# A GRU step on one Trainium2 core: gates r and z in banks of their own, fp32 products for the newest terms, and fp32 moving operands of 4 columns

## The reference

```
def step(h, xs):
    xzt, xrt, xht = xs
    z = jax.nn.sigmoid(xzt + h @ U_z + vz)
    r = jax.nn.sigmoid(xrt + h @ U_r + vr)
    hh = jnp.tanh(xht + r * h @ U + vh)
    h_new = (1.0 - z) * h + z * hh
    return (h_new, h_new)
h0 = jnp.zeros((seq.shape[0], U.shape[0]), seq.dtype)
xs = (jnp.swapaxes(xz, 0, 1), jnp.swapaxes(xr, 0, 1), jnp.swapaxes(xh, 0, 1))
_, out_t = jax.lax.scan(step, h0, xs)
```

## Time and profile before

| What | us |
|---|---|
| median of 3 runs | 760.3 |
| span of the profiled execution, first to last instruction | 755.7 |
| median of the runs less that span | 4.6 |
| PE busy, of that span | 640.4 |
| DVE busy | 461.1 |
| ACT busy | 324.6 |
| POOL busy | 178.0 |

### The profile page before, as it was taken

The page is one execution under the profiler, slowest core; times in us unless marked ns, Lnnn a source line. Parts: engine busy times, 40 slices in busy tenths (PEclk is TensorE's granted clock), DMA queues, the critical chain, the costliest instruction groups (busy, mean ns, idle before and its releaser), DMA issues.

```text
span 755.7 us, 26078 instructions
## 1 busy us (share of the span) xinstructions
PE 640.4 (85%) x7909; PEld 528.5 (70%) x7909; DVE 461.1 (61%) x3362; ACT 324.6 (43%) x1253; POOL 178.0 (24%) x789
## 2 busy tenths in 40 slices
PE   5998677656788888988889898889888889999995
PEld 4445566545677877877778787778777667877774
DVE  1536344343267777777777777777767556777663
ACT  2356434434145546455555555464544222322321
POOL 1023222221033232232232332322311001111110
PEclk9999967899589999999999999999999999999997
DMA  8022222222212221222212221212210000000000
GB/s 221 9 85 76 85 88 79 92 79 79 76 40 67 74 69 65 67 71 68 71 64 65 74 64 65 74 64 67 72 62 3 2 2 2 10 6 3 4 6 8
DMA packets 43965, 43.06 MB, mean 57 GB/s; under 512 B 5500, under 2 KB 43656, under 8 KB 43784
## 3 DMA queue, kind: packets, MB, share of 16 engines
q1 hardware_dynamic: 43328, 40.75, 16.6%
q10 hardware_dynamic: 584, 1.64, 0.6%
HBM read 20.95 MB, written 21.43 MB: 56 GB/s over the span
## 4 chain that ended last, share of the span: by engine, by line
PE 54%; DVE 14%; DMA 14%; issue 9%; ACT 7%; SPq 1%; DVEq 1%; ACTq 0%; POOLq 0%; POOL 0%
DMA skew<-e_sb 13%; PE bank L622 12%; PE bank L635 12%; PE bank L423 7%; PE bank L407 6%; DVE s_sb L845 3%; ACT hh L765 3%; PE bank L440 2%; DVE g L996 2%; DVE q L988 2%; ACT oT L651 2%; PE bank L455 2%; PE bank L527 2%; PE bank L457 2%; PE bank L453 2%
## 5 line engine op out<-in xcount | busy, mean ns | idle before, releaser
L355 POOL COPY x_nat<-d 128x4 f32 (+1 forms) x256 | 53.5, 209 | 395.7 <-DVE d L1001 395.7
L635 PE MATMUL bank<-q,uc 128*128 128x54 f32 (+1 forms) x512 | 106.1, 289 | 43.3 <-DVE q L988 40.8
L635 PEld LDWEIGHTS bank<-q,uc 128*128 128x128 f32 x512 | 77.7, 190 | 90.3 <-DVE q L988 85.6
L622 PE MATMUL bank<-g,uw 128*128 128x54 f16 (+1 forms) x2560 | 119.1, 189 | 3.6 <-DVE g L996 3.6
L755 ACT ACTIVATE trz<-bank 128x8 f32<-128x8 f32 x256 | 45.5, 178 | 167.9 <-PE bank L622 167.6
L622 PEld LDWEIGHTS bank<-g,uw 128*128 128x128 bf16 x2560 | 103.6, 97 | 17.1 <-DVE g L996 7.9
L622 PE MATMUL bank<-b,uw 128*128 128x54 f16 (+1 forms) x2560 | 110.1, 188 | 0.0
L651 ACT ACTIVATE e_sb<-bank 128x132 f32<-128x132 f32 (+1 forms) x256 | 84.2, 382 | 57.6 <-DMA skew<-e_sb 55.5
L622 PEld LDWEIGHTS bank<-b,uw 128*128 128x128 bf16 x2560 | 108.1, 103 | 1.0 <-issue 0.2
L765 ACT ACTIVATE hh<-bank 128x4 f32<-128x4 f32 x256 | 44.5, 174 | 135.7 <-PE bank L635 131.3
L996 DVE TENSOR_TENSOR g<-z,hh 128x4 f16<-128x4 f32 x256 | 41.9, 164 | 97.5 <-ACT hh L765 97.5
(11 more groups left out here) (133 smaller groups left out, 1054.4 us busy)
## 6 DMA issues: line engine op xcount, KB each, us to landing
skew<-e_sb SPq DMA_DIRECT2D x128, 159.5 KB, 2.7
pos<-skew SPq DMA_DIRECT2D x128, 128.0 KB
wkv_sb<-in_L_attn_Wkv ACTq DMA_DIRECT2D x1, 1024.0 KB, 8.3
x_nat<-in_x SPq DMA_DIRECT2D x1, 512.0 KB, 4.6
wq_sb<-in_L_attn_Wq ACTq DMA_DIRECT2D x1, 512.0 KB, 5.3
wo_sb<-in_L_attn_Wo SPq DMA_DIRECT2D x1, 512.0 KB, 7.3
out<-y_out SPq DMA_DIRECT2D x8, 64.0 KB
ffn_nat<-in_L_ffn_w_gate SPq DMA_DIRECT2D x1, 256.0 KB
```

The costliest lines, as they stand in the source:

```text
L622: ins = mm(out_, uw[:, gate, use, j, :], operand, start=False, stop=True, skip_group_check=True)
L635: mm(c_cols(k, n), uc[:, :], st["q8"][:, now, 0:n], start=False, stop=True, skip_group_check=True).then_inc(c_pre, 1)
```

## The change

Gate r now lies in bank 0, gate z in bank 1, the candidate in bank 2, for all 16 steps of a period. Gate z is one fp32 product of its U with the whole state d8. Gate r is five fp16 products of the older term b as before, and one fp32 product with g8. g1 and g2 are gone, with their two DVE instructions; tanh is taken of r and z apart, each with its own semaphore. The moving operands of the three fp32 products of a step (g8, d8, q8) have 4 columns, while the five products with b keep 54 or 60. The zero products go to bank 2, with widths as before. The setting of a bank to its biases (seed) is split in three and placed between the DVE instructions of a step, and input products of r and z are issued between the products with b and `first_window`.

```diff
-        parts = sb("parts", [128, 2, 3, D], BF16)
-        uw = sb("uw", [128, 2, 2, 3, D], BF16)
+        parts = sb("parts", [128, 3, D], BF16)
+        uw = sb("uw", [128, 3, D], BF16)
+        u32 = sb("u32", [128, 2, D])
...
-        def rz_cols(k, gate=0, n=2 * B):
-            at = (k % BLOCK * 2 + gate) * B
-            return bank[k // BLOCK][:, at:at + n]
-        def c_cols(k, n=B):
-            return bank[2][:, k * B:k * B + n]
+        def pre_cols(gate, k, n=B):
+            return bank[gate][:, k * B:k * B + n]
...
-                    for use, name, ok in ((1, "b", (b1_ok, b2_ok)), (0, "g", (g1_ok, g2_ok))):
-                        if name == "g":
-                            first_window(i, k, groups, tiles, last)
-                        for low in range(2):
-                            pe.wait_ge(ok[low], t + 1)
-                            for gate in range(2):
-                                ins = product(rz_cols(k, gate, n), gate, use, st[f"{name}{low + 1}"][:, before, 0:n], low)
-                    ins.then_inc(rz_pre, 1)
+                    NR, NZ, NC = B, B, B
+
+                    pe.wait_ge(b1_ok, t + 1)
+                    for j in range(3):
+                        mm(pre_cols(0, k, n), uw[:, j, :], st["b1"][:, before, 0:n], start=False, stop=True, skip_group_check=True)
+                    pe.wait_ge(b2_ok, t + 1)
+                    for j in range(2):
+                        mm(pre_cols(0, k, n), uw[:, j, :], st["b2"][:, before, 0:n], start=False, stop=True, skip_group_check=True)
+                    gate_inputs(i, k, last)
+                    first_window(i, k, groups, tiles, last)
+                    pe.wait_ge(g8_ok, t + 1)
+                    mm(pre_cols(0, k, NR), u32[:, 0, :], st["g8"][:, before, 0:NR], start=False, stop=True,
+                       skip_group_check=True).then_inc(r_pre, 1)
+                    pe.wait_ge(d8_ok, t + 1)
+                    mm(pre_cols(1, k, NZ), u32[:, 1, :], st["d8"][:, before, 0:NZ], start=False, stop=True,
+                       skip_group_check=True).then_inc(z_pre, 1)
                     main_window(i, k, groups, tiles, last)
                     pe.wait_ge(q8_ok, t + 1)
-                    mm(c_cols(k, n), uc[:, :], st["q8"][:, now, 0:n], start=False, stop=True, skip_group_check=True).then_inc(c_pre, 1)
+                    mm(pre_cols(2, k, NC), uc[:, :], st["q8"][:, now, 0:NC], start=False, stop=True, skip_group_check=True).then_inc(c_pre, 1)
...
-                    act.wait_ge(rz_pre, t + 1)
-                    act.activation(trz[:, now, :, :].rearrange("p g b -> p (g b)"), rz_cols(k), ACT.Tanh, scale=0.5).then_inc(trz_ok, 1)
+                    act.wait_ge(r_pre, t + 1)
+                    act.activation(trz[:, now, 0, :], pre_cols(0, k, B), ACT.Tanh, scale=0.5).then_inc(tr_ok, 1)
+                    act.wait_ge(z_pre, t + 1)
+                    act.activation(trz[:, now, 1, :], pre_cols(1, k, B), ACT.Tanh, scale=0.5).then_inc(tz_ok, 1)
```

More of the change, by code:

```diff
@@ L593, in main_window, with gate_inputs @@
                 if not groups[0][0]:
-                    free = bank[1 - k // BLOCK] if k not in (1, 9) else bank[3] if groups[1][0] else bank[7]
                     n = FILLER // 2 if any(s_ in TILE_MAIN for _, s_ in tiles_at(i, k, tiles)) else FILLER
-                    mm(free[:, 0:n], uw[:, 0, 0, 0, :], zeros[:, 0:n], start=(k in (1, 9)), stop=True, skip_group_check=True)
+                    mm(bank[2][:, 0:n], uw[:, 0, :], zeros[:, 0:n], start=False, stop=True, skip_group_check=True)
+                if k == 4:
+                    inputs(i, 1, 2)
+                if k == 15 and not last:
+                    inputs(i + 1, 0, 2)
+            def gate_inputs(i, k, last):
                 if k == 2:
@@ L599, in main_window @@
                     inputs(i, 1, 0)
+                if k == 3:
                     inputs(i, 1, 1)
-                if k == 4:
-                    inputs(i, 1, 2)
                 if k == 14 and not last:
@@ L764, in period @@
                     act.wait_ge(c_pre, t + 1)
-                    act.activation(st["hh"][:, now, :], c_cols(k), ACT.Tanh).then_inc(hh_ok, 1)
+                    act.activation(st["hh"][:, now, :], pre_cols(2, k), ACT.Tanh).then_inc(hh_ok, 1)
             periods(act, period)
@@ L817, in _ @@
             for n, item in enumerate(KQV):
-                if n % 2 == 1 and n // 2 < 13:
+                if n % 2 == 1 and n // 2 < 8:
                     split_u(n // 2)
@@ L973, in window @@
                     tile_stage(tau, step)
-                if k == 1 or (k == 9 and not last):
-                    seed(0 if k == 9 else 1)
             def period(i, groups, tiles, last):
@@ L983, in period @@
                     tr, tz = trz[:, now, 0, :], trz[:, now, 1, :]
-                    d8 = st["d8"][:, before, :]
+                    d8 = st["d8"][:, before, 0:B]
                     stt = dve.scalar_tensor_tensor
-                    dve.wait_ge(trz_ok, t + 1)
+                    dve.wait_ge(tr_ok, t + 1)
                     dve.wait_ge(d8_ok, t + 1)
                     stt(s["q8"], tr, 1.0, d8, ALU.add, ALU.mult).then_inc(q8_ok, 1)
+                    seeds = k == 1 or (k == 9 and not last)
+                    if seeds:
+                        seed(0 if k == 9 else 1, 0)
+                    dve.wait_ge(tz_ok, t + 1)
+                    dve.tensor_scalar(s["z8"], tz, 1.0, SPLIT, ALU.add, ALU.mult).then_inc(z8_ok, 1)
+                    stt(s["b8"], tz, -1.0, d8, ALU.add, ALU.mult).then_inc(b8_ok, 1)
                     stt(s["b1"], tz, -1.0, d8, ALU.add, ALU.mult).then_inc(b1_ok, 1)
-                    stt(s["b8"], tz, -1.0, d8, ALU.add, ALU.mult).then_inc(b8_ok, 1)
-                    dve.tensor_scalar(s["z8"], tz, 1.0, SPLIT, ALU.add, ALU.mult).then_inc(z8_ok, 1)
+                    if seeds:
+                        seed(0 if k == 9 else 1, 1)
                     dve.wait_ge(b8_ok, t + 1)
+                    dve.wait_ge(b1_ok, t + 2)
                     dve.tensor_tensor(s["b2"], s["b8"], s["b1"], ALU.subtract).then_inc(b2_ok, 1)
```

72 lines of the change are left out of this document (32 added, 40 removed).

## The result

The changed kernel takes 1008.97 us in the median of 4 runs (1007.1 to 1009.98), the kernel before 761.01 us in its 4 (759.01 to 762.62): a ratio of 1.3276, 95% interval [1.3237, 1.3316]. The profiled execution has a span of 1005.3 us.

What follows compares the result with a forecast made beforehand. Before, late steps were bound by the chain, with DVE also holding odd steps beside attention. At 1.2 GHz, 204.8 + 572.0 + 212.0 + 14.2 = 1003 us of span, with 4.6 us more 1008 us; range 850 to 1070.

Steps and rivals of the forecast that it cites:

- The clock: In the recurrence: starts at 1.2 GHz and, with the change, doesn't rise to 2.4 GHz, or not for long; chance 0.74.
- The count of columns: On PE: a recurrence step streams 1296 columns before, 318 after; with attention beside it, 3,080 become 2,100.
- the first rival: In the recurrence: the clock stays at or comes back to 2.4 GHz and the kernel is faster, 712 us; chance 0.10.
- the cold entry: At the recurrence's start: either kernel enters at 1.2 GHz, since attention runs dry ahead of it.
- slower steps keep the clock low: In the recurrence: steps at 1.2 GHz are slower and so emptier, against the clock holding beside attention.
- The price at 1.2 GHz: In the recurrence: 3.25 us a step beside attention and 2.65 late, for a span of 1003 us.
- heads, projection and inputs: On PE beside attention: 6.8 us a period, some 1 us of it in gaps, adding 0.36 us a step.
- PE sets the steps: Beside attention at 1.2 GHz: PE's own work is longer than the 2.12 us chain, 3.23 us odd, 2.58 even.
- the price of the first rival: In the recurrence at 2.4 GHz: 16 us less in late steps, 32 us less beside attention, from 760.3 to 712 us.
- I take nothing: On ACT beside attention: the second tanh, from nothing to 0.18 us a step, is put at no cost.
- the cover for z's tanh and b2: Behind r's product: z's tanh and its DVE readers are covered by the 0.43 us to the candidate's tanh; late b2 costs nothing.
- the other end: On ACT beside attention: the second tanh's upper cost, 176 x 0.18 = 32 us.

Runs made afterwards that it cites:

- e1: The changed kernel with its three fp32 moving operands 54 or 60 columns wide again: 811.53 us, 1.0677 of the kernel before.
- e3: The kernel before with all its operands 4 columns wide instead of 54 and 60: 919.08 us, 1.2131 of the kernel before.
- e6: As e5, with the three fp32 moving operands 54 or 60 columns wide again: 778.25 us, 1.0239 of the kernel before.
- e7: The kernel before with operands of 27 and 30 columns, half as wide: 784.39 us, 1.0322 of the kernel before.
- e5: The changed kernel with zero products ahead of the recurrence, in even steps beside attention and late steps, two more in each of the first six: 1055.36 us.
- e9: The changed kernel with z's and b's operands 100 or 128 wide, zero products at entry and in the first six steps, work reordered: 792, 822, 821, 762 us.
- e10: As e9, with three products of zeros in one more step, ahead of a PE wait for ACT: 763.32 us, 1.0043 of the kernel before.
- e4: The changed kernel with 20 products of zeros, 512 wide, ahead of the recurrence and none in it: 1009.57 us, 1.3321 of the kernel before.
- e8: The changed kernel with a fourth 4-column fp32 product per step, on zeros, ahead of r's product: 1108.65 us, 1.459 of the kernel before.
- e12: As e10, with ACT's copies of e_sb moved ahead of z's tanh: 757.56 us, 0.9954 of the kernel before; the six shorter runs have 754.6 us.
- e11: The kernel before with only the candidate's operand 4 wide; products with g 54, with b 54, 90 or 100: 753.83 us, 0.9934 of the kernel before.

## Why the prediction was right

**The clock** was the step that decided, and it held: 0.50 from the start of the recurrence to its end. Its reason, that what streams through the array tells stretches apart and the busy share doesn't, is borne out by e1, e3, e6 and e7: same rows, other widths, another clock. The count of columns itself doesn't order the two structures, though: counted as the prediction does, e1_wide streams 5 x 54 + 3 x 4 x 54 + 1,780 = 2,700 a step beside attention and e7_before_half 24 x 27 + 1,780 = 2,430, but it is e1_wide whose clock is down for whole stretches there (0.73 from 204.5 to 244, 0.79 from 283 to 325), where e7_before_half has 0.99 from 420 to 550. What the clock follows is thus shown for the width within a structure, and is open beyond that.

The rule that the first rival came from (the Trainium skill, "TensorE: Matmul & The Clock Gate", section "HAM oscillation — how this bites in real kernels": the clock falls where PE idles between bursts) doesn't explain a clock that stays low: rows cover 99% of 785 us at 1.2 GHz. What the array does inside a row isn't seen, and waits may have a part in the fall itself: in e5 and e9 it comes within 2 us of a wait of PE of 0.35 and 0.56 us. By themselves such waits don't do it, for the kernel before has ten waits for oT of up to 0.8 us in its attention part and e10 has the same one of 0.56 us, at 2.4 GHz. The part of the reason that spoke of the cold entry was idle, by e4. That slower steps keep the clock low is what e5 fits, since it falls there once and for all; no run tests it by itself, and e9 came back after 75 us.

**The price at 1.2 GHz** held term by term: 3.25 us forecast and 3.25 measured beside attention, 2.65 and 2.68 late, head and tail within 0.5 us. Over all steps beside attention the odd ones take 3.60 us and the even ones 2.89, which is the forecast's 3.23 and 2.58 with 0.37 and 0.31 on top, where it had put 0.36 on both for heads, projection and inputs. The odd step in the timeline takes 3.19. That the sum came within 1 us of 1009 is partly luck: 0.8 too much beside attention, 2.5 too little late, 0.5 too little in the head and 0.9 too much for what the median has beside the span (3.7, not 4.6) nearly cancel, and 3.25 and 2.65 were taken by judgment from 3.27 and 2.61. The ends of the range were added up wrongly, without effect: they should read 918 and 1072, not 919 and 1076. The even step has a part that follows the chain, where load to hh reads 0.63 us as forecast, in the changed kernel's timeline:

```profile
456.11 0.50 PEld L634 LDWEIGHTS bank<-q,uc 128*128 128x128 f32 x2 [0.18 <-DVE q L986]
...
456.74 0.17 ACT L766 ACTIVATE hh<-bank 128x4 f32<-128x4 f32 x1 [0.24 <-PE bank L634]
```

**That PE sets the steps** is shown by e8 for all that stands ahead of r's product. Behind it an even step follows the chain, as worked out (1.06 us) and as the rows above show.

**What was wrong is the price of the first rival.** It had 712 us with the clock kept; the kernels that keep it take 754.6 (e12), 762.8 (e10) and 778 (e6). None of them is the changed kernel with another clock: they have wider operands or more zeros, e10 and e12 have work in other places, and all have 3 to 6 us more head. Late steps came as worked out, 1.71 us where they are quiet, but 8 us in all instead of 16, since other late steps are held by the expert tile and the inputs, one of them at 1.96 us (639.83 to 641.79). The step that failed is "I take nothing" for ACT's second tanh and, with it, the cover for z's tanh and b2. Its reason was misread: the 181 us are all that ACT does, its tanhs too, and say nothing of what stands ahead of hh. Beside attention 32 us were to be gained; e10 lost 7 and e12 broke even, so even the other end (32 us of cost) was too low for e10. It is also the even steps, not the odd ones, in which q8 waits for DVE's pass over the scores: in the kernel before the pass at 386.08 holds q8 (386.43) in the step that has the product of positions at 385.21. In place of the term put at nothing there are waits that the chain of a late step doesn't show. One is the second tanh beside ACT's copies, by e10 and e12. Another is seen in e6_more_zeros_wide, where b2 ends at about 386.8 and PE waits with all that is queued behind its products:

```profile
386.64 0.16 DVE L1007 TENSOR_TENSOR b<-b 128x4 f16<-128x4 f32 x1
...
386.86 0.22 PE L627 MATMUL bank<-b,uw 128*128 128x54 f16 x2
...
387.05 0.16 DVE L1010 TENSOR_TENSOR g<-z,hh 128x4 f32<-128x4 f32 x1 [0.25 <-ACT hh L775]
...
387.13 0.68 PE L420 MATMUL bank<-v_sb,pt_sb 128*128 x4
...
387.65 0.33 PE L636 MATMUL bank<-g,u 128*128 128x54 f32 x2
```

r's product starts 0.44 us after g8 is done (387.21), behind the values. The seed copies and the input products in that window are a third, seen in e1_wide, where a step became 2.6 us long for them (e10 and e12 have these products elsewhere). In a late step of e1_wide's timeline, PE's wait for the seed and r's product behind it:

```profile
729.40 0.40 PE L521 MATMUL bank<-x1T,wx 128*128 x2 [0.35 <-DVE bank L905]
...
730.11 0.33 PE L627 MATMUL bank<-g,u 128*128 128x60 f32 x2
```

How the missing 32 us divide among the three isn't measured, beyond the 7 net of ACT's order. With the clock held, the 712 us would have been 43 to 51 us too low, 3 to 6 of them for the longer head.

## What to carry to other kernels

Before the filling columns of a moving operand are cut, read the granted clock and ask what else streams there: their length costs 0.04 us for a product on the chain, and the clock that they hold up is worth 160 us. Narrow only the operand on the chain and put the width on products that nobody waits for. That is worth little here, 0.7% (e11), but it is steady. A step that is split so that one gate comes earlier brings the other one later, so look at what is queued behind the later one, on ACT and on PE, and not at the chain alone.

## What the runs showed that was not expected

- One program can run the same kind of steps at either clock: e5 ran some 18 steps at 2.4 GHz and then 780 us at 1.2 GHz.
- Entering a stretch at full clock buys nothing if the stretch can't hold it (e4, 1009.6 against 1009.0 us).
- Moving ACT's copies ahead of z's tanh shortened odd steps by 0.16 us and lengthened even ones by 0.08 (e12 against e10).
- Width had little price in an fp32 product at full clock: load to hh is 0.47 us with 60 columns and 0.43 with 4. At 1.2 GHz a product of 4 columns adds 0.39 us to a step that PE sets (e8).
- Three products of zeros in one step went with a clock held in nine of ten runs (e10, 758 to 764 us), where without them three of four were at 792 or more (e9); four runs are few.
